# Issuing two loads earlier in the SyncE queue of a gated cross-attention kernel

## What is computed

```python
# _L0_xattn_ref, SIZE 512, HEADS 16, HEAD_DIM 32
q = einsum('oc,bct->bot', Wq, target) + bq[None, :, None]
k = einsum('oc,bcs->bos', Wk, source) + bk[None, :, None]
v = einsum('oc,bcs->bos', Wv, source) + bv[None, :, None]
dot = einsum('bhdt,bhds->bhts', q, k) / sqrt(HEAD_DIM)
mask = target_mask[:, :, :, None] * source_mask[:, :, None, :]
dot = mask * dot - (1.0 - mask) * NEG
out = einsum('bhts,bhds->bhdt', softmax(dot, axis=-1) * mask, v)

# reference, x is (8, 512, 1024), ctx (8, 512, 1024)
x = x + tanh(g_xattn[0]) * xattn(_layernorm(x), ctx, mask, mask, Wq, bq, Wk, bk, Wv, bv)
x = x + tanh(g_ffn[0]) * ffn(_layernorm(x), W2, scale, scale1)   # q1, q2 rounded to float8, then a matmul
```

## Time and profile before

| what | value |
|---|---|
| time, median of 3 runs | 2628.47 us (2626.02 to 2632.49) |
| the profiled execution: its time, its span | 2626.02 us, 2624.2 us |
| TensorE (PE) busy | 2522.7 us, 96% of the span |
| VectorE (DVE) busy | 1976.4 us, 75% |
| GpSimd (POOL) busy | 1652.3 us, 63% |
| ScalarE (ACT) busy | 1425.9 us, 54% |
| moved by queue q1 | 265.80 MB |

### The profile page before, as it was taken

The page is one execution under the profiler, slowest core; times in us unless marked ns, Lnnn a source line. Parts: engine busy times, 40 slices in busy tenths (PEclk is TensorE's granted clock), DMA queues, the critical chain, the costliest instruction groups (busy, mean ns, idle before and its releaser), DMA issues.

```text
span 2624.2 us, 41111 instructions
## 1 busy us (share of the span) xinstructions
PE 2522.7 (96%) x13425; PEld 1399.5 (53%) x13425; DVE 1976.4 (75%) x3251; ACT 1425.9 (54%) x2638; POOL 1652.3 (63%) x1265
## 2 busy tenths in 40 slices
PE   5999999978999999999999999999999999999995
PEld 4888888864444444444444444444444444444441
DVE  5766666637788888888888787888888888888763
ACT  2333333322666666666666666666666666666663
POOL 1433333423777777777777777777777777777774
PEclk8999999997999999999999999999999999999997
DMA  6666666654333334444443343333333444443311
GB/s 210 232 237 235 235 238 235 229 166 87 76 76 84 92 85 90 97 95 96 96 89 84 87 92 84 84 84 84 92 84 88 97 97 94 97 91 84 88 34 41
DMA packets 208249, 306.12 MB, mean 117 GB/s; under 512 B 41240, under 2 KB 108888, under 8 KB 208064
## 3 DMA queue, kind: packets, MB, share of 16 engines
q1 hardware_dynamic: 195920, 265.80, 40.1%
q10 hardware_dynamic: 12144, 38.02, 4.1%
HBM read 200.09 MB, written 102.11 MB: 115 GB/s over the span
## 4 chain that ended last, share of the span: by engine, by line
PE 66%; DVE 6%; issue 3%; POOL 1%; DMA 1%; ACT 0%; DVEq 0%; SPq 0%; POOLq 0%; ACTq 0%
PE s_bank L694 19%; PE o_bank L720 18%; PE x_bank L707 16%; PE d_bank L731 7%; DVE part_max L872 5%; PE x_bank L755 4%; PE x_bank L746 1%; POOL pair_sum L965 1%; PE x_bank L738 1%; DVE y L103 1%; DMA q_st<-qx_scr 0%; DVE isnan L102 0%; POOL y L974 0%; ACT probs L800 0%; DVE neg_max L886 0%
## 5 line engine op out<-in xcount | busy, mean ns | idle before, releaser
L965 POOL TENSOR_TENSOR pair_sum<-probs 128x512 f32<-128x512 f32 x1024 | 1284.1, 1285 | 494.1 <-ACT probs L800 494.1
L872 DVE TENSOR_REDUCE part_max<-x_bank 128x1 f32<-128x512 f32 x2048 | 1280.7, 683 | 377.3 <-PE x_bank L707 370.2
L800 ACT ACTIVATE probs<-s_bank 128x512 f32<-128x512 f32 x2048 | 1071.5, 603 | 645.4 <-PE s_bank L694 638.7
L694 PE MATMUL s_bank<-q_st,k_st 100*128 100x512 f32 x2048 | 875.4, 429 | 4.7 <-ACT probs L800 4.7
L707 PE MATMUL x_bank<-k_st,q_st 98*128 98x512 f32 x2048 | 823.5, 406 | 25.1 <-DMA q_st<-qx_scr 21.5
L694 PEld LDWEIGHTS s_bank<-q_st,k_st 100*128 100x128 f32 x2048 | 387.1, 189 | 510.0 <-issue 264.1
L720 PE MATMUL o_bank<-probs,v_t 128*32 128x512 f32 x4096 | 545.5, 605 | 0.0
L707 PEld LDWEIGHTS x_bank<-k_st,q_st 98*128 98x128 f32 x2048 | 392.4, 192 | 143.6 <-DMA q_st<-qx_scr 22.0
L731 PE MATMUL d_bank<-pair_sum,ones 128*32 128x512 f32 x2048 | 266.6, 592 | 2.8 <-POOL pair_sum L965 2.8
L322 POOL TENSOR_TENSOR stage_lo<-stage,stage_hi 128x512 fp32r<-128x512 f32 x128 | 186.5, 1481 | 121.8 <-ACT stage_hi L392 121.2
L392 ACT ACTIVATE stage_hi<-stage 128x512 fp32r<-128x512 f32 x128 | 79.8, 632 | 190.9 <-DVE stage L476 142.1
(11 more groups left out here) (99 smaller groups left out, 2085.2 us busy)
## 6 DMA issues: line engine op xcount, KB each, us to landing
k_st<-k_scr SPq DMA_DIRECT2D x96, 512.0 KB
q_st<-q_scr SPq DMA_DIRECT2D x192, 256.0 KB
c_raw<-in_ctx_dram ACTq DMA_DIRECT2D x32, 512.0 KB, 6.6
x_raw<-in_x_dram ACTq DMA_DIRECT2D x32, 512.0 KB, 6.2
k_scr<-stage_hi SPq DMA_DIRECT2D x64, 256.0 KB, 2.4
k_scr<-stage_lo SPq DMA_DIRECT2D x64, 256.0 KB, 2.6
v_scr<-stage SPq DMA_DIRECT2D x64, 256.0 KB, 2.7
q_scr<-stage_hi SPq DMA_DIRECT2D x64, 256.0 KB, 2.1
```

Source lines behind the costliest of these rows:

```text
L694: nc.tensor.matmul(s_bank_of(n, k)[:, :], k_st[p][0:KS, h, j * P:(j + 1) * P], q_st[p][0:KS, th, h, :], start=True, stop=True).then_inc(sc ...
L800: nc.scalar.activation(probs[:, c % PR, h, :], s_bank_of(n, k)[:, :], ACT.Exp).then_inc(exp_done, 1)
L872: nc.vector.tensor_reduce(part_max[:, th, sh, at:at + 1], x_bank_of("tile", k)[:, :], AX, ALU.max).then_inc(max_done, 2)
L965: nc.gpsimd.tensor_tensor(pair_sum[:, r % 2, h], probs[:, a, h], probs[:, a + 1, h], ALU.add).then_inc(pair_done, 1)
```

## The change

SyncE's stream of a period is written in another order. `load_res(n-1)` moves from behind `move_den(n-1, 1)` to ahead of it, and `load_v(n+1)` moves from behind `load_tm(n)` to the same place. Both now stand directly behind `stack(n+1)`. Waits, sizes, buffers and all other engines' streams are the same.

```diff
                         if real(n + 1):
                             stack(n + 1, 1 - p)
                         if real(n - 1):
+                            load_res(n - 1, 1 - p)
+                        if real(n + 1):
+                            load_v(n + 1, 1 - p)
+                        if real(n - 1):
                             move_den(n - 1, 1)
-                            load_res(n - 1, 1 - p)
                             move_inv(n - 1, 1)
                         if real(n):
                             set_max(n, 1, p)
...
                         if real(n):
                             load_tm(n)
-                        if real(n + 1):
-                            load_v(n + 1, 1 - p)
                         if real(n):
                             move_den(n, 0)
```

## The result

The changed kernel takes 2691.35 us, the median of six runs (2679.65 to 2695.24); the kernel before takes 2628.31 us beside it. The ratio is 1.023, with a 95% interval of 1.021 to 1.025. That is slower, as forecast, inside the range, and 15 us above the 2676 us that I named. The profiled execution of the changed kernel took 2675.94 us, the fastest of the seven timed here; its span is 2674.1 us, 49.9 us longer than the span before. Its time varies by more than that of the kernel before (2626.02 to 2632.49); how much of that the clock can account for is worked out at the end.

What follows compares the result with a forecast made beforehand. TensorE was taken to bound the kernel, busy 61.1 of each 61.9 us period. A stall of 30 x 1.64 = 49 us on 2626.02 us gave 2675, named as 2676 us against the runs' median (1.8% slower); range 2625 to 2712.

Steps and rivals of the forecast that it cites:

- The bound and what the edit takes away: Attention stage: TensorE busy 61.1 of 61.9 us a period; no engine waits for `res` or `v_t`, so earlier loads gain 0.
- `den_c` lands with `v_t`: SyncE's queue: `res` lands at 1562.5, `v_t` and with it `den_c` 2.2 us later, at 1564.7; bounds 1563.6 to 1567.3.
- the order of one queue: SyncE's queue: a later DMA is served behind earlier ones, so `den_c` waits for the 1 MB ahead of it.
- The stall: TensorE, waiting for VectorE's late reductions, loses 2.3 - 0.5 - 0.2 = 1.6 us in each of 30 periods.
- D: VectorE's wait for `den_c` before the reciprocal, from 1562.43 to 1564.7: 2.3 us in each of 30 periods.
- the dearer stall: Rival, 0.06: TensorE loses 4.2 us a period (126 us, 2752 us), or its clock falls, costing another 75 us.
- What is queued behind: SyncE's moves after `den_c`: `set_max` and `inv_b` go out 2.3 us later, still in time; at most 0.5 us gained.
- `den_c` in time: Rival, 0.13: `den_c` still lands before VectorE needs it, so no change, 2626 to 2630 us.
- Faster: Rival, 0.05: the stretch freed of `v_t` traffic shortens periods, at most 25 us, more likely a third: 2618 us.

Runs made afterwards that it cites:

- The third load: The changed kernel with one more 512 KB load, into a buffer nobody reads, between `load_v` and `move_den`: 2746.72 us, ratio 1.044.

## Why the prediction was right, and where not

**The bound and what the edit takes away.** Right. TensorE had nothing to spare, the earlier `res` and `v_t` gained nothing, and no wait for either appeared.

**`den_c` lands with `v_t`.** Right in the changed kernel. I forecast it 24.6 us after the stack's first DMA; VectorE took it up after 1591.73 - 1567.87 = 23.9 us. The load of `res` issued at 1573.09 shows which term was too large:

```profile
DMA to landing us min/median/max: 16.9/16.9/16.9
```

`res` lands at 1573.09 + 16.9 = 1590.0, 22.1 us after the stack's first DMA, where I had 22.4; `v_t` lands 1.5 us behind it, and not 2.2. The third load cost 1.5 us as well. Both loads behind it: no cost; one ahead: 0 to 0.2%; a third ahead: 1.5 us more. The reason given, the order of one queue, is only part of it, as `den_c` is also late on a queue of its own while the DMA engines have the stack and 1 MB to serve. The Trainium skill (DMA: Bandwidth & Descriptors, Queues, rings and completion order) says that a DMA engine takes turns between queues, packet by packet; a move in many small pieces would then be held up at each turn. No row here shows the turns.

**The stall.** The step that failed is its composition. I took D = 2.3 us of waiting for `den_c`; it was 1.3 us. I counted L900 as the 0.35 us of the earlier trace rows; behind a late `den_c` it takes up to 1.35 us. Removing it gave back 42 us while the wait stayed. The reductions of slot 24 started 1593.20 - 1590.25 = 2.95 us after VectorE was free for the reciprocal in the period shown, against 1563.53 - 1562.43 = 1.1 before: 1.85 us late, where I had worked out 1.8. Two errors cancelled there. TensorE's loss by waiting was 34.6 / 30 = 1.15 us a period, against my 1.64: 1.6 to 1.8 us in 15 periods, and 0.4 to 0.6 in the 15 in which L900 ended with the addition before.

**The clock.** I gave the dearer stall, with the clock as one of its forms, 0.06. It did happen, behind seven of the 15 longer stalls and none of the 15 shorter ones, and made up about 10 of the 49.9 us in the profiled execution. It explains the spread only in part. The profiled execution has a mean clock of 0.977 and 2674.1 us; those with spans of 2688 to 2693 us have 0.971 to 0.974. The longest, 2693.4 us, has 0.974: the lower level held for some 16 us more than in the profiled one, which costs 8 us at most (an estimate from the mean clocks), and it is 19 us longer. A larger share of the longer stalls could be the rest, but there is no trace of that execution. The kernels with short stalls (one load alone, L900 removed) show no fall, the one with the longest (2.8 us of waiting) shows them in each of its 30 periods. My argument that 2 us of idle time are too short for it was wrong.

**What is queued behind.** Right: no wait at slot 32, for `max_rows` or `inv_b`. I did not foresee that the issue of `den_c` itself takes up to 2.8 us on SyncE, in place of 0.56 us; 1.89 us of it stand in the period above. Nothing waited for SyncE there.

**The rivals.** `den_c` in time: refuted by 30 waits. Faster: refuted. In sum the forecast of 49 us met the profiled 49.9 us by luck: its stall was too large for half of the periods, and the 10 us of the clock were missing. No version tried beats the kernel before; three of the variants equal it.

## What to carry to other kernels

Ahead of a small DMA on which a compute engine has a deadline, count the bytes that are queued, whatever their own deadlines: an early load is free only behind such a move. A reader in the trace that has never waited may have 1 us to spare or 10; put one transfer ahead of it and look. And where TensorE sets the pace, price a short, repeated stall at more than its length, for the clock may fall behind it.

## What the runs showed of the hardware

- VectorE's small L900 (128 x 16 elements) ends 0.03 to 0.04 us after one of GpSimd's additions ends, in 61 of its 64 executions in the changed kernel, stalled or not: it is held for as long as the addition runs, up to 1.35 us for 0.23 us of work. The delay that it hands on comes in steps of one addition, 1.5 or 2.7 us here, however late `den_c` is within the step. The Trainium skill (SBUF — State Buffer, Who interferes with whom) says that the two engines share a pair of ports, that VectorE needs it for a second SBUF input and for `tensor_scalar` in some modes, and that the loser is blocked for the whole instruction. The trace agrees with it in the held `SCALAR_TENSOR_TENSOR` and `TENSOR_SCALAR` and in the reciprocal that is never held.
- Behind 1.6 to 1.8 us in which TensorE stood, the granted clock fell (0.57 on average over the next 4 us) in 7 of 15 periods; behind 0.4 to 0.6 us it fell in none of 15. The times of the kernel, in six runs each, scattered by 15.6 us, against 6.5 before.
- A move of 8 KB took 9.2 to 10.5 us to land behind the stack and 1 MB on one queue, and 9.2 to 10.4 us on a queue of its own (in the 18 periods in which it came late) while the other queue held these, against 1.86 us on idle DMA engines.
